# Layers 2 and 3 with value products between the first score blocks, and two of layer 2's expert products formed in layer 1's FFN

## The chip, the cores and the metric

One NeuronCore of one Trainium2 chip runs the whole program as one launch. The metric is the device time of that launch in microseconds, the median of several runs. A core has five engines, each with its own program, which meet only through semaphores: PE (TensorE, matrix products, results to PSUM), ACT (ScalarE), DVE (VectorE), POOL (GpSimd) and SP (SyncE, which here issues the DMAs). The profile lists PE's weight loads apart, as PEld.

## What is computed

The input x holds 8 sequences of 112 tokens with 256 features (896 tokens, 7 tiles of 128). Four layers follow, each a cross-attention to a context of 8 x 375 keys with 192 features and then a feed-forward network (FFN), both behind a layer norm and added to x:

```python
x = x + _L1_xattn_ref(_layernorm(x), ctx, ...)      # 8 heads of 128
x = x + _L1_ffn_ref(_layernorm(x), ...)             # quantised gate, up and down
x = x + _L2_xattn_ref(_layernorm(x), ctx, ...)      # 16 heads of 64
x = x + _L2_ffn_ref(_layernorm(x), ...)             # 8 experts, the best two of each token
x = x + _L3_xattn_ref(_layernorm(x), ctx, ...)      # 16 heads of 64
x = x + _L3_ffn_ref(_layernorm(x), ...)             # 8 experts and a shared one
```

An expert of layer 2 has nothing between its two matrices, so their product doesn't depend on x:

```python
for e in range(E):
    h = xt @ w_in[e].T
    y = y + gates[:, e:e + 1] * (h @ w_out[e].T)
```

The attention of layers 2 and 3 is q = xn Wq, k = c Wk, v = c Wv, softmax(q k^T / 8) v Wo, head by head.

## The kernel before

The program is a row of phases: attention and FFN of layers 0, 1, 2, 3. Each phase ends with a barrier of all engines, and the next begins behind it. Inside a phase an engine's instructions stand in a fixed order, written out by hand. Products that need more than one pass of precision are split in a high and a low part (names that end in H and L), with three to five matmuls for one product: ACT copies the high part out of PSUM, DVE subtracts it to get the low part.

**Layer 1's FFN** (`layer1_ffn`, L1399). DVE computes the layer norm of the 7 tiles, scales and rounds them to `f_xq`; PE turns them (L1550, 14 transposes), ACT copies them out (L1514). Then, tile by tile, PE forms the gate and up products (`up`, L1554, bf16, 8 matmuls of 512 columns in banks 0 to 3), ACT applies silu (L1521), DVE multiplies and finds the maximum (L1475, L1478), ACT scales (L1526), DVE rounds (L1491), PE turns the result (L1566), ACT copies it out (L1531), PE forms the down product (`down`, L1562, in banks 6 and 7 by turns) and DVE adds it to x (L1496). PE's order is up(i+1), down(i-1) for each i; ACT's is gates(i+1), scaled(i), turned_out(i-1). No DMA and no POOL instruction is in this phase.

**Attention of layers 2 and 3** (`attention_heads64`, L1581, called for both). Heads go in 8 pairs h, and in a pair one sequence b after another: 64 steps (h, b), numbered n = 8h + b. For one step PE forms the scores of both heads (L1895, into banks 0 and 1, which every step reuses), DVE the maximum (L2062), ACT the exponentials with their sums (L1976), DVE the reciprocals (L2067), POOL the normalised probabilities (`norm`, L1774); PE turns them (L1905), ACT and DVE take the high and low part out (L1982, L2071), PE multiplies by the values (mix, 9 matmuls) and ACT and DVE take the result out (L1990, L2080). In step n PE issues scores(n+3), turn(n+1), pieces of other work, and mix(n).

The pieces are what step tables (L1594 to L1600) assign: chunks of keys (5 matmuls of 500 columns), halves of queries (6 of 448), units of values (10 of 256; 12 units u for two head pairs), output products, and in layer 2 the products of the experts (`combine`, L1878: 8 matmuls of 128x256 in plain float32 for half an expert (e, j); DVE copies the result, L2055). All of these share three PSUM banks by turns: the m-th piece waits until DVE has emptied the bank of piece m-3. The experts stand in the even head pairs, two each, at steps 1, 3, 5 and 7. The values of head pair 0 stand in steps 0 to 6:

```python
EXPERTS_AT = {1: (0, 0), 3: (0, 1), 5: (1, 0), 7: (1, 1)} if experts else {}
FIRST_VALUES_AT = (None, None, 0, 1, 1, 2, 3, 3, 4, 5, 5, 6)
```

Ahead of the steps stands the start of the phase. SP loads the weights of pair 0 (L1748), POOL cuts them in high and low parts (L1808), DVE computes the layer norm, PE forms five key chunks, with the turning of the normed x between the third and the fourth, then values(0,0), queries(0,0), values(0,1), scores of steps 0, 1 and 2 (L1948), turn(0); then step 0. The queries' second half, (0,1), stands in step 0, and scores of step 4 need it.

**Layer 2's FFN** uses the 8 products `combined` that the attention has left.

## Time and profile before

| what | us |
|---|---|
| median of 3 runs | 1965.8 (1965.56 to 1965.81) |
| the profiled execution | 1964.94 |
| its span in the trace | 1963.1 |
| layer 1's FFN, first instruction of DVE to that of the next phase | 982.1 to 1039.1 |
| layer 2's attention, to its last normalisation | 1039.1 to 1426.2 |
| layer 3's attention, to its last normalisation | 1495.7 to 1826.7 |

Times inside the trace are microseconds from the start of the span; busy time of PE is a modelled end, so matmuls that follow each other overlap, and the start of one to the start of the next is what it costs. PEclk is the clock that the chip granted to TensorE, as a share of 2.4 GHz (0.50 is 1.2 GHz). A timeline row gives start, duration, engine, line, operation, result <- operands, and in brackets the idle time of the engine before it with what ended that.

### The profile page before, as it was taken

How to read it: one execution, taken by the hardware profiler on the slowest of the kernel's cores; microseconds unless marked ns; L12 is line 12 of the kernel's file. 1: busy time of each engine (PE TensorE's matmuls, PEld its weight loads, DVE VectorE, ACT ScalarE, POOL GpSimd, SP SyncE). 2: the span in 40 equal slices, each digit the busy share in tenths (PEclk: the TensorE clock that was granted, in tenths of full speed). 3: DMA queues.
4: the chain of work that ended last, by engine and by line, in shares of the span. 5: the costliest groups of instructions: out<-in, count | busy, mean ns of one | idle time of the engine just before them, and what ended most of it. 6: DMA issues, size and time to landing. Idle time of an engine off the chain costs nothing. (4 is left out here: it accounts for less than half of the span.)

```text
span 1963.1 us, 33822 instructions
## 1 busy us (share of the span) xinstructions
PE 1793.0 (91%) x11747; PEld 1588.6 (81%) x11750; DVE 1420.3 (72%) x3161; ACT 1020.1 (52%) x2243; POOL 507.3 (26%) x533
## 2 busy tenths in 40 slices
PE   6858999999999999999857999999967999999698
PEld 6637999899898989899725888888856888888587
DVE  6478787777777777778676576766676677777786
ACT  3345656465564555656454464655522666666421
POOL 0514030302111120302003233333342334333342
PEclk9988999999999999999978999999989999999899
DMA  4011000000000000000001202020100000000011
GB/s 157 1 75 33 1 12 1 4 8 0 11 0 11 0 11 0 3 0 1 1 1 60 82 28 94 15 94 20 47 1 27 9 15 23 9 10 4 23 54 40
DMA packets 17591, 48.43 MB, mean 25 GB/s; under 512 B 2602, under 2 KB 7347, under 8 KB 15796
## 3 DMA queue, kind: packets, MB, share of 16 engines
q1 hardware_dynamic: 16596, 45.99, 7.1%
q8 instruction: 67, 1.10, 0.2%
...
## 5 line engine op out<-in xcount | busy, mean ns | idle before, releaser
L1280 ACT ACTIVATE a_pH<-banks 125x512 fp32r<-125x512 f32 (+1 forms) x384 | 203.5, 543 | 272.9 <-PE banks L195 192.5
L1351 DVE TENSOR_TENSOR a_pL<-banks,a_pH 125x512 fp32r<-125x512 f32 (+1 forms) x384 | 235.3, 623 | 100.2 <-ACT a_pH L1280 96.5
L1774 POOL TENSOR_TENSOR a_prob<-a_prob,a_rinv 112x750 f32<-112x750 f32 x128 | 183.9, 1437 | 433.7 <-DVE a_rinv L2067 433.7
L1327 DVE TENSOR_SCALAR_CACHE_REDUCE a_prob<-banks 128x500 f32<-128x500 f32 x336 | 223.0, 677 | 17.1 <-issue 12.1
L1181 PE MATMUL banks<-ident,a_prob 128*125 128x128 f32 x1344 | 201.5, 274 | 6.6 <-ACT a_prob L1265 4.4
L195 PE MATMUL banks<-a_pH,a_head_vH 125*128 125x256 f32 (+1 forms) x576 | 203.3, 353 | 2.1 <-DVE a_pL L1351 1.1
L1265 ACT ACTIVATE a_prob<-a_prob,a_nmax 128x1000 f32<-128x1000 f32 x168 | 188.0, 1122 | 28.2 <-DVE a_nmax L1330 28.2
L1181 PEld LDWEIGHTS banks<-ident,a_prob 128*125 128x125 f32 x1344 | 186.9, 188 | 9.9 <-ACT a_prob L1265 4.9
L1137 POOL TENSOR_TENSOR a_head_oH<-a_o,ones 128x256 fp32r<-128x256 f32 (+1 forms) x24 | 16.4, 685 | 624.5 <-DVE a_o L1360 624.5
L195 PE MATMUL banks<-a_pH,a_head_vL 125*128 125x256 f32 (+1 forms) x576 | 173.0, 300 | 0.0
L195 PE MATMUL banks<-a_pL,a_head_vH 125*128 125x256 f32 (+1 forms) x576 | 172.8, 300 | 0.0
L1982 ACT ACTIVATE a_pH<-banks 125x672 fp32r<-125x672 f32 x128 | 93.8, 733 | 128.8 <-PE banks L1905 128.8
L2062 DVE TENSOR_REDUCE a_nmax<-banks 112x2 f32<-112x750 f32 x128 | 119.5, 934 | 45.7 <-PE banks L1895 45.7
L1976 ACT ACTIVATE a_prob<-banks,a_nmax 112x375 f32<-112x375 f32 x256 | 143.8, 572 | 11.9 <-DVE a_nmax L2062 11.9
L195 PE MATMUL banks<-a_head_kH,a_head_qH 128*128 128x500 f32 x336 | 134.6, 401 | 10.8 <-DVE a_prob L1327 9.5
L195 PE MATMUL banks<-a_head_kL,a_head_qH 128*128 128x500 f32 x336 | 131.2, 390 | 0.0
L195 PE MATMUL banks<-a_head_kH,a_head_qL 128*128 128x500 f32 x336 | 130.9, 390 | 0.0
L2071 DVE TENSOR_TENSOR a_pL<-banks,a_pH 125x672 fp32r<-125x672 f32 x128 | 109.8, 858 | 29.1 <-ACT a_pH L1982 27.9
L1905 PEld LDWEIGHTS banks<-ident,a_prob 112*125 112x125 f32 x768 | 95.8, 192 | 33.3 <-issue 33.0
L1990 ACT ACTIVATE a_oH<-banks 64x112 fp32r<-64x112 f32 x256 | 66.0, 258 | 107.2 <-PE banks L195 105.1
L1905 PE MATMUL banks<-ident,a_prob 112*125 112x112 f32 x768 | 118.7, 292 | 0.5 <-DVE a_pL L2071 0.5
L195 PEld LDWEIGHTS banks<-a_pH,a_head_vH 125*128 125x128 f32 x576 | 108.7, 189 | 8.0 <-DVE a_pL L1351 5.2
...
## 6 DMA issues: line engine op xcount, KB each, us to landing
a_w_out<-in_f_out SPq DMA_DIRECT2D x8, 1024.0 KB, 4.9
a_w_in<-in_f_in SPq DMA_DIRECT2D x16, 512.0 KB, 4.7
...
f_quant_raw<-in_f_w SPq DMA_DIRECT2D x3, 1024.0 KB, 7.8
...
```

The costliest lines, as they stand in the source:

```text
L195: last = pe.matmul(out, a, b, start=start and n == 0, stop=stop and n == len(terms) - 1)
L1181: last = pe.transpose(TB[c % 4][0:KB, at:at + P], prob[:, t % RING, key:key + KB], s.ident[:])
L1265: act.activation(row, row, ACT.Exp, bias=nmax[:, t % RING:t % RING + 1], accum_out=rsum[:, t % RING, n:n + 1]).then_inc(exp_done, 1)
L1280: act.activation(pH[:, c % RING, 0:wide], TB[c % 4][0:KB, 0:wide], ACT.Copy).then_inc(t_high, 1)
L1327: dve.tensor_scalar(prob[:, at, c * CHUNK:(c + 1) * CHUNK], SB[c % 3][:, 0:CHUNK], SCALE, None, ALU.mult, ALU.max, accum_out=chunk_max[:, ...
L1351: dve.tensor_tensor(pL[:, c % RING, 0:wide], TB[c % 4][0:KB, 0:wide], pH[:, c % RING, 0:wide].bitcast(F32), ALU.subtract).then_inc(t_done, 1)
L1774: pool.tensor_tensor(both, both, rinv[:, n % RING, :].unsqueeze(2).to_broadcast([SEQ, 2, KEYS]), ALU.mult).then_inc(p_normed, 1)
L1905: last = pe.transpose(T[0:KB, at // BKT, (at % BKT) * SEQ:(at % BKT + 1) * SEQ], probs(n, i)[:, k * KB:(k + 1) * KB], s.ident[0:SEQ, 0:SEQ])
L1976: last = act.activation(probs(n, i), S[0:SEQ, i, own_keys(n % BATCH)], ACT.Exp, bias=nmax[:, n % RING, i:i + 1], accum_out=rsum[:, n % RIN ...
L1982: act.activation(pH[:, n % 2, :].rearrange("p (i c) -> p i c", i=2), T[0:KB, :, 0:HALF], ACT.Copy)\
L2062: dve.tensor_reduce(nmax[:, n % RING, :], S[0:SEQ, :, own_keys(n % BATCH)], AX.X, ALU.max, negate=True).then_inc(max_ready, 1)
L2071: dve.tensor_tensor(pL[:, n % 2, :].rearrange("p (i c) -> p i c", i=2), T[0:KB, :, 0:HALF], pH[:, n % 2, :].rearrange("p (i c) -> p i c", ...
```

## The change

Four things.

1. In both attentions the value units 2 to 9 of head pair 0 leave steps 0 to 5 and stand between the first score blocks: scores(0), three units, scores(1), one unit, turn(0), two units, scores(2), two units. ACT's and DVE's programs follow, DVE with `one_over_sums(0)` behind two low parts. Units 10 and 11 stand in steps 3 and 4.
2. The products of experts 6 and 7 are formed in layer 1's FFN. SP loads both matrices of expert 6 (2 MB) at the start of that phase and those of expert 7 when PE is through with 6. PE forms expert 6's product (16 matmuls) ahead of the transposes of `f_xq`, and expert 7's in four pieces of 4 matmuls, between up(i+1) and down(i-1) for i = 1 to 4. Both use bank 7, ACT copies them out, and layer 1's down product uses bank 6 alone. Head pair 6 of layer 2's attention has no experts any more.
3. The weights of head pair 0 are loaded and cut ahead of the phase that uses them: layer 2's in layer 1's FFN, layer 3's as a ninth pair at the end of layer 2's attention (cut at steps 1 and 2 of pair 7, the values at step 7 of pair 6).
4. `combined` lives from layer 0 on, and the quantised weights of layer 1 lie in its first part.

```diff
@@ -1438,7 +1438,28 @@
+        first_loaded, first_high, first_cut = sem("f1_first_loaded"), sem("f1_first_high"), sem("f1_first_cut")
+        w_in = sb("f1_w_in", [P, KT, EXPERTS, P])
+        w_out = sb("f1_w_out", [P, EXPERTS, D])
+        expert_loaded, e_filled, e_done = sem("f1_expert_loaded"), sem("f1_e_filled"), sem("f1_e_done")
+        EARLY = range(EXPERTS - 2, EXPERTS)
+        PIECE = EXPERTS // 2
...
+        @block.sync
+        def _(sp):
+            for n, e in enumerate(EARLY):
+                if n > 0:
+                    sp.wait_ge(e_filled, KT * n)
+                sp.dma_start(w_out[:], dram["f2_out"][e]).then_inc(expert_loaded, 16)
+                for j in range(KT):
+                    sp.dma_start(w_in[:, j, :, :], dram["f2_in"][e, j]).then_inc(expert_loaded, 16)
+                if n == 0:
+                    first_weights_load(sp, s.pair, dram, 2, first_loaded)
+        @block.gpsimd
+        def _(pool):
+            first_weights_cut(pool, s.pair, first_loaded, first_high, first_cut)
@@ -1493,7 +1514,7 @@
-                dve.scalar_tensor_tensor(s.x[:, i, :], B[6 + i % 2][:, 0:D], ha[:, 3, i:i + 1], s.x[:, i, :],
+                dve.scalar_tensor_tensor(s.x[:, i, :], B[6][:, 0:D], ha[:, 3, i:i + 1], s.x[:, i, :],
@@ -1507,8 +1528,14 @@
+            def combined(n, j):
+                act.wait_ge(e_filled, KT * n + j + 1)
+                act.activation(s.combined[:, EARLY[n], j * D:(j + 1) * D], B[7][:, 0:D], ACT.Copy).then_inc(e_done, 1)
...
+            for j in range(KT):
+                combined(0, j)
@@ -1536,12 +1563,26 @@
+                if i in (3, 5):
+                    combined(1, (i - 3) // 2)
...
+            def combine(n, j, part):
+                pe.wait_ge(expert_loaded, 48 * n + 48)
+                need(pe, e_done, KT * n + j)
+                for k in range(PIECE * part, PIECE * part + PIECE):
+                    last = pe.matmul(B[7][:, 0:D], w_in[:, j, k, :], w_out[:, k, :], start=k == 0, stop=k == EXPERTS - 1)
+                if part == 1:
+                    last.then_inc(e_filled, 1)
+            for j in range(KT):
+                for part in range(2):
+                    combine(0, j, part)
@@ -1566,19 +1607,55 @@
-                need(pe, y_added, i - 1)
-                split_products(pe, B[6 + i % 2][:, 0:D], [
+                need(pe, y_added, i)
+                split_products(pe, B[6][:, 0:D], [
                     (hqT[:, i % 2, k, :], w_down[:, k, :]) for k in range(IT)]).then_inc(y_filled, 1)
...
+                if 1 <= i <= 4:
+                    combine(1, (i - 1) // 2, (i - 1) % 2)
...
+def first_weights_load(sp, w, dram, layer, loaded):
+    sp.dma_start(w.qk_raw[:], dram[f"a{layer}_qk"][0]).then_inc(loaded, 16)
+    sp.dma_start(w.wv_raw[:], dram[f"a{layer}_wv"][0]).then_inc(loaded, 16)
+def first_weights_cut(pool, w, loaded, high, cut):
+    pool.wait_ge(loaded, 32)
+    pool.tensor_copy(w.wH[:], w.qk_raw[:]).then_inc(high, 1)
+    pool.tensor_copy(w.wvH[:], w.wv_raw[:]).then_inc(high, 1)
+    pool.wait_ge(high, 2)
+    pool.tensor_tensor(w.wL[:], w.qk_raw[:], w.wH[:].bitcast(F32), ALU.subtract).then_inc(cut, 1)
+    pool.tensor_tensor(w.wvL[:], w.wv_raw[:], w.wvH[:].bitcast(F32), ALU.subtract).then_inc(cut, 1)
...
@@ -1597,7 +1674,7 @@
-    FIRST_VALUES_AT = (None, None, 0, 1, 1, 2, 3, 3, 4, 5, 5, 6)
+    FIRST_VALUES_AT = {10: 3, 11: 4}
@@ -1613,12 +1690,14 @@
-            return [(0, u) for u, at in enumerate(FIRST_VALUES_AT) if at == b]
+            return [(0, u) for u, at in FIRST_VALUES_AT.items() if at == b]
...
+    LATE = EXPERTS - 2
     def experts_at(h, b):
-        return [(h + EXPERTS_AT[b][0], EXPERTS_AT[b][1])] if h % 2 == 0 and b in EXPERTS_AT else []
+        return [(h + EXPERTS_AT[b][0], EXPERTS_AT[b][1])] if h % 2 == 0 and h < LATE and b in EXPERTS_AT else []
@@ -1632,7 +1711,9 @@
     count("v", (0, 0))
     count("q", (0, 0))
-    count("v", (0, 1))
+    for u in range(1, UNITS):
+        if u not in FIRST_VALUES_AT:
+            count("v", (0, u))
...
@@ -1745,25 +1826,24 @@
-            qk(0)
-            values(0)
             sp.dma_start(bias[:], dram[f"a{layer}_bias"]).then_inc(bias_loaded, 16)
             outs(0)
             if experts:
                 expert(0, 0)
             qk(1)
+            values(1)
             for h in range(HEADS):
                 for b in range(BATCH):
-                    if b == 3 and h + 2 < HEADS:
+                    if b == 3 and h + 2 < PAIRS:
                         qk(h + 2)
-                    if b == 0 and h % 2 == 0 and h // 2 + 1 < HEADS // 2:
-                        values(h // 2 + 1)
+                    if b == 2 and h % 2 == 1 and h // 2 + 2 < (PAIRS + 1) // 2:
+                        values(h // 2 + 2)
                     if b == 4 and h + 1 < HEADS:
                         outs(h + 1)
                     for e, j in experts_at(h, b):
                         if j == 0:
                             expert(e, 1)
@@ -1805,9 +1882,6 @@
-            cut_keys(0)
-            cut_values(0)
-            cut_queries(0)
@@ -1819,13 +1893,13 @@
                         norm(n + 2)
-                    if b == 1 and h + 1 < HEADS:
+                    if b == 1 and h + 1 < PAIRS:
                         cut_keys(h + 1)
-                    if b == 2 and h + 1 < HEADS:
+                    if b == 2 and h + 1 < PAIRS:
                         cut_queries(h + 1)
                     if b == 3 and h >= 1:
                         cut_outs(h)
-                    if b == 7 and h % 2 == 0 and h // 2 + 1 < HEADS // 2:
+                    if b == 7 and h % 2 == 0 and h // 2 + 1 < (PAIRS + 1) // 2:
                         cut_values(h // 2 + 1)
 
@@ -1945,9 +2019,17 @@
             values(0, 1)
-            for b in range(AHEAD):
-                scores(0, b)
+            scores(0, 0)
+            for u in (2, 3, 4):
+                values(0, u)
+            scores(0, 1)
+            values(0, 5)
             turn(0)
+            for u in (6, 7):
+                values(0, u)
+            scores(0, 2)
+            for u in (8, 9):
+                values(0, u)
             for h in range(HEADS):
                 for b in range(BATCH):
@@ -2111,11 +2201,20 @@
             queries(0, 0)
             values(0, 1)
-            for b in range(AHEAD):
-                maxima(b)
-                if b < 2:
-                    one_over_sums(b)
+            maxima(0)
+            for u in (2, 3):
+                values(0, u)
+            one_over_sums(0)
+            values(0, 4)
+            maxima(1)
+            values(0, 5)
             turned(0)
+            one_over_sums(1)
+            for u in (6, 7):
+                values(0, u)
+            maxima(2)
+            for u in (8, 9):
+                values(0, u)
             dve.wait_ge(bias_added, 1)
             for h in range(HEADS):
@@ -2434,17 +2533,17 @@
         s.xnTL = ctx.enter_context(nc.sbuf_tensor("xnTL", [P, KT, TOK], F32R))
-        with ExitStack() as quantised:
-            s.w_quant = quantised.enter_context(nc.sbuf_tensor("w_quant", [P, 3, 2048], BF16))
-            s.w_mean = quantised.enter_context(nc.sbuf_tensor("w_mean", [P, 3], F32))
-            layer0_ffn(nc, s, dram)
-            layer1_attention(nc, s, dram)
+        s.combined = ctx.enter_context(nc.sbuf_tensor("combined", [P, EXPERTS, KT * D], F32))
+        s.w_quant = s.combined[:].rearrange("p e c -> p (e c)").bitcast(BF16)[:, 0:3 * 2048].rearrange("p (n c) -> p n c", n=3)
+        s.w_mean = ctx.enter_context(nc.sbuf_tensor("w_mean", [P, 3], F32))
+        layer0_ffn(nc, s, dram)
+        layer1_attention(nc, s, dram)
+        with ExitStack() as pairs:
+            s.pair = PairWeights(nc, pairs)
             layer1_ffn(nc, s, dram)
-        with ExitStack() as combined:
-            s.combined = combined.enter_context(nc.sbuf_tensor("combined", [P, EXPERTS, KT * D], F32))
-            attention_heads64(nc, s, dram, 2, experts=True)
+            attention_heads64(nc, s, dram, 2, following=3, experts=True)
             layer2_ffn(nc, s, dram)
-        attention_heads64(nc, s, dram, 3)
+            attention_heads64(nc, s, dram, 3)
```

At the start of layer 1's FFN, PE's order before (`f_xq` is the rounded x, `w_quant` the quantised weights):

```order
L1550 MATMUL banks<-f_ident,f_xq 128x128 x14
L195 MATMUL banks<-w_quant,f_xqT 128x512 x24
L1566 MATMUL banks<-f_ident,f_hq 128x128 x8
L195 MATMUL banks<-w_quant,f_hqT 128x256 x8
L195 MATMUL banks<-w_quant,f_xqT 128x512 x8
L1566 MATMUL banks<-f_ident,f_hq 128x128 x8
```

and PE's order there now (the quantised weights go by the name `combined`):

```order
L1579 MATMUL banks<-f_w_out,f_w_in 128x256 x16
L1591 MATMUL banks<-f_ident,f_xq 128x128 x14
L195 MATMUL banks<-combined,f_xqT 128x512 x24
L1579 MATMUL banks<-f_w_out,f_w_in 128x256 x4
L1607 MATMUL banks<-f_ident,f_hq 128x128 x8
L195 MATMUL banks<-combined,f_hqT 128x256 x8
L195 MATMUL banks<-combined,f_xqT 128x512 x8
L1579 MATMUL banks<-f_w_out,f_w_in 128x256 x4
L1607 MATMUL banks<-f_ident,f_hq 128x128 x8
```

Expert 6's 16 matmuls stand ahead of everything, and four of expert 7 ahead of the transposes of each of the first four tiles' hidden values.

At the start of layer 2's attention, DVE's order before, from the maximum of scores(0) on (`a_vL` is a value unit's low part, `a_pL` that of the turned probabilities, `a_qL` that of the queries):

```order
L2062 TENSOR_REDUCE a_nmax<-banks 112x2
L2067 RECIPROCAL a_rinv<-a_rsum 112x2
L2062 TENSOR_REDUCE a_nmax<-banks 112x2
L2067 RECIPROCAL a_rinv<-a_rsum 112x2
L2062 TENSOR_REDUCE a_nmax<-banks 112x2
L2071 TENSOR_TENSOR a_pL<-banks,a_pH 125x672
L2067 RECIPROCAL a_rinv<-a_rsum 112x2
L2062 TENSOR_REDUCE a_nmax<-banks 112x2
```

and DVE's order there now:

```order
L2152 TENSOR_REDUCE a_nmax<-banks 112x2
L2134 TENSOR_TENSOR a_vL<-banks,a_vH 125x512 x2
L2157 RECIPROCAL a_rinv<-a_rsum 112x2
L2134 TENSOR_TENSOR a_vL<-banks,a_vH 125x512
L2152 TENSOR_REDUCE a_nmax<-banks 112x2
L2134 TENSOR_TENSOR a_vL<-banks,a_vH 125x512
L2161 TENSOR_TENSOR a_pL<-banks,a_pH 125x672
L2157 RECIPROCAL a_rinv<-a_rsum 112x2
L2134 TENSOR_TENSOR a_vL<-banks,a_vH 125x512 x2
L2152 TENSOR_REDUCE a_nmax<-banks 112x2
L2134 TENSOR_TENSOR a_vL<-banks,a_vH 125x512 x2
L2157 RECIPROCAL a_rinv<-a_rsum 112x2
```

Eight low parts of values now stand between the maxima and reciprocals of the first three steps.

## Rows read from the trace of the kernel before

**Rows 1.** Windows: busy time of each engine, then granted clock, DMA.

```profile
982.00:1038.00 56.00, 28.77 (x179) 15.96 (x182) 42.05 (x111) 28.61 (x39) 0.00 (x0) 0.79 0.00 1
1000.00:1002.00 2.00, 2.00 (x10) 0.76 (x9) 1.49 (x3) 1.00 (x3) 0.00 (x0) 0.96 0.00 0
1056.84:1074.35 17.51, 11.34 (x61) 9.23 (x62) 7.25 (x12) 7.78 (x21) 4.31 (x3) 0.71 0.01 1
1110.00:1390.00 280.00, 279.21 (x1950) 247.29 (x1949) 184.73 (x361) 157.09 (x421) 94.20 (x90) 1.00 0.17 55
1513.80:1531.50 17.70, 11.54 (x63) 9.40 (x63) 7.26 (x12) 7.76 (x21) 4.31 (x3) 0.71 0.00 0
```

**Rows 2.** Timeline of POOL: normalisations of steps 32 and 48, layers 2 and 3.

```profile
1251.93 1.44 POOL L1774 TENSOR_TENSOR a_prob<-a_prob,a_rinv 112x750 f32<-112x750 f32 x1 [4.60 <-DVE a_rinv L2067]
1344.88 1.44 POOL L1774 TENSOR_TENSOR a_prob<-a_prob,a_rinv 112x750 f32<-112x750 f32 x1 [4.61 <-DVE a_rinv L2067]
1678.65 1.44 POOL L1774 TENSOR_TENSOR a_prob<-a_prob,a_rinv 112x750 f32<-112x750 f32 x1 [4.16 <-DVE a_rinv L2067]
1757.32 1.44 POOL L1774 TENSOR_TENSOR a_prob<-a_prob,a_rinv 112x750 f32<-112x750 f32 x1 [4.16 <-DVE a_rinv L2067]
```

**Rows 3.** Timeline of PE in layer 1's FFN.

```profile
993.96 0.59 PE L1550 MATMUL banks<-f_ident,f_xq 128*128 128x128 bf16 x4 [13.55 <-DVE f_xq L1463]
1009.91 1.89 PE L195 MATMUL banks<-w_quant,f_hqT 128*128 128x256 bf16 x8 [1.12 <-ACT f_hqT L1531]
1026.69 1.89 PE L195 MATMUL banks<-w_quant,f_xqT 128*128 128x512 bf16 x7
1030.59 1.05 PE L195 MATMUL banks<-w_quant,f_hqT 128*128 128x256 bf16 x8 [1.57 <-ACT f_hqT L1531]
```

**Rows 4.** Timeline of ACT in layer 1's FFN, one tile.

```profile
1027.32 1.26 ACT L1521 ACTIVATE f_gate<-banks,f_xa 128x512 f32<-128x512 f32 x2 [1.57 <-PE banks L195]
1029.52 1.02 ACT L1531 ACTIVATE f_hqT<-banks 128x1024 bf16<-128x1024 bf16 x1
```

**Rows 5.** DMA issues of 1096 to 1106 us: KB, us to landing.

```profile
a_w_out<-in_f_out SPq DMA_DIRECT2D x1, 1024.0 KB, 5.0
a_w_in<-in_f_in SPq DMA_DIRECT2D x1, 512.0 KB, 6.0
```

**Rows 6.** Timelines of DVE and POOL: layer norms of two phases.

```profile
982.24 2.38 DVE L96 BATCH_NORM_STATS2 f_ln_stats<-x_stream 128x6 f32<-128x256 f32 x7
986.55 2.35 DVE L118 TENSOR_SCALAR f_xn<-x_stream,f_ln_mean_var,f_ln_root 128x256 f32<-128x256 f32 x7
...
1039.09 2.39 DVE L96 BATCH_NORM_STATS2 a_ln_stats<-x_stream 128x6 f32<-128x256 f32 x7 [0.91 <-PEq L61]
1043.48 1.28 POOL L1798 TENSOR_TENSOR a_wvL<-a_wv_raw,a_wvH 128x512 fp32r<-128x512 f32 x1
1043.58 1.20 DVE L109 SCALAR_TENSOR_TENSOR a_ln_root<-a_ln_root 128x7 f32<-128x7 f32 x1
1045.15 2.84 DVE L118 TENSOR_SCALAR a_prob<-x_stream,a_ln_mean_var,a_ln_root 128x256 f32<-128x256 f32 x7
```

**Rows 7.** Timeline of PE at the start of layer 2's attention.

```profile
1048.69 1.69 PE L164 MATMUL banks<-ident,a_prob 128*128 128x128 f32 x14
...
1056.84 0.42 PE L1895 MATMUL banks<-a_kH,a_qH 64*112 64x376 f32 x2
...
1060.32 0.42 PE L1895 MATMUL banks<-a_kH,a_qH 64*112 64x376 f32 x2 [2.72 <-ACT a_prob L1976]
...
1072.08 0.28 PE L195 MATMUL banks<-a_wvH,ctxH 128*125 128x256 f32 x1
...
1073.26 0.27 PE L195 MATMUL banks<-a_pH,a_vH 125*128 125x224 f32 x1
```

**Rows 8.** Timelines of ACT and DVE there: one value unit taken out.

```profile
1073.46 0.60 ACT L1961 ACTIVATE a_vH<-banks 125x512 fp32r<-125x512 f32 x1 [0.63 <-PE banks L195]
1074.09 0.69 DVE L2044 TENSOR_TENSOR a_vL<-banks,a_vH 125x512 fp32r<-125x512 f32 x1 [0.61 <-ACT a_vH L1961]
```

75 lines of the change are left out of this document (45 added, 30 removed).

## Prediction

> **What bounds the kernel now.** I read the windows by stage first. In the middle of layer 2's attention PE is busy 279.2 of 280 us at clock 1.00 [rows 1]: there PE sets the time, and a matmul taken out is time gained. The start of each attention is of another kind. From layer 2's first scores to those of step 4 PE is busy 11.34 of 17.51 us at mean clock 0.71, and layer 3's start shows the same, 11.54 of 17.70 [rows 1]: 6.2 us idle, and as a mean of 0.71 says that 58% of the stretch ran at 1.2 GHz instead of 2.4, some 3.6 us more go to half speed (3.3 if idle and busy time were evenly mixed). The timeline of PE says why: scores(1) start 3.48 us behind scores(0), after 2.72 us idle for ACT's exponentials [rows 7], since all scores share one pair of banks. Layer 1's FFN is the third kind: PE is busy 28.8 of 56 us and DVE 42.1, in chains through all engines, and POOL and DMA do nothing [rows 1]. So the change moves work from where PE is full to where it has room, and the question is what it costs there.
>
> **Part 1, products in layer 1's FFN: a loss.** SP starts the 2 MB of expert 6 with the phase, at about 982.1 (DVE's norm begins at 982.24 [rows 6]). The nearest transfers, 1 MB and 0.5 MB, landed 5.0 and 6.0 us after their issues, and the second was issued some 0.4 us later, so 0.5 MB takes about 1.4 us; 2 MB land at 982.1 + 6.4 + 1.4 = 989.9 [rows 5].
>
> What does a product cost? Two equal blocks of two head pairs, in layer 2 with experts and in layer 3 without, take 1344.88 - 1251.93 = 92.95 and 1757.32 - 1678.65 = 78.67 us [rows 2]. All else in them is the same work, so four half-expert products of 8 matmuls cost 14.28, and one 3.57, at full clock. In the FFN the first meets a PE that has been idle for 13.55 us [rows 3]. Before, PE began there at 993.96 [rows 3] and had full clock only from 1000.1 on (mean 0.96 in the window from 1000 [rows 1]), with gaps in its work. The products leave no gap; between 0 and 6.1 us of half speed I take 3, which lose 1.5. Product one ends at 989.9 + 3.57 + 1.5 = 995.0. The second waits for ACT to copy bank 7, at most the 0.60 of its 512-column copies [rows 8], and ends at 999.2. The transposes that began at 993.96 begin 5.4 us later with a hand-over; from 4 (no half speed) to 8 (6.1 us of it).
>
> Then the loop over tiles. At full clock it takes 4.78 us and runs up 1026.69, silu 1027.32, scaling, turned copy 1029.52 to 1030.54, down product 1030.59 to 1031.47 [rows 3, 4]. PE's own way through it is up and transposes 1030.59 - 1026.69 - 1.57 = 2.33, then 1.1 for ACT's copy behind them, then down 0.88: 4.3. Four matmuls of expert 7 (half of 3.57, 1.79) between up and transposes make it 6.1, longer than the loop: 1.3 us each for i = 2, 3, 4. At i = 1 the piece lies in the wait for DVE's rounding. So +3.9. At i = 3 the piece also waits for ACT's copy of the half before it, which stands behind silu and scaling of the next tile: 0.63 + 2.2 + 0.4 behind up's start, where up itself takes 1.7: +1.5. ACT's copy at i = 5 stands ahead of the turned copy: +0.4. Against that a busier PE keeps its clock: a down product of 8 matmuls took 1.89 at 1009.91 and 1.05 at 1030.59 [rows 3], and it, the up product behind it and the transposes ahead of both would lose 2.5 us less. The loop costs 3.9 + 1.5 + 0.4 - 2.5 = +3.3. Down products in bank 6 alone cost nothing: DVE's addition of 256 columns, under the 0.69 that it took for 512 [rows 8], is done while PE turns the next tile and ACT copies it. Expert 7's load starts at 999.2 and lands some 8 us later, ahead of its first piece at about 1011. **Layer 1's FFN: 5.4 + 3.3 = +8.7**, bounds +6 and +14 (both halves half as dear again).
>
> POOL's cut of the first weights moves here as well, to about 991 to 995, where DVE scales and rounds x. In layer 2's norm a DVE instruction on 7 columns took 1.20 us beside POOL's subtraction of 1.28, and ended with it [rows 6]. With 1.28 for each of two subtractions and half that, an estimate, for each of two copies, DVE could be held up by 3.8 us in all, and `f_xq`, for which PE waited until 993.96 [rows 3], come at 997.8. PE isn't through with expert 6 until 999.2: cost nothing, and up to 3.8 if that cover were gone. The Trainium skill (SBUF — State Buffer, "SBUF: two separate sides") calls the port pair of DVE and GpSimd an exclusive lock for which the loser waits a whole instruction; the trace agrees. By it the moved cut is no cheaper in the FFN than in the attention, only better covered, and the sum stays as it is.
>
> **Part 2, weights ahead: a gain at both starts.** From its first to its last instruction the norm takes 982.24 to 988.90, 6.66 us, with POOL silent, and 1039.09 to 1047.99, 8.90 us, beside POOL's cuts [rows 6]: 2.2 us go. PE's first key chunks no longer wait for a cut, so the turning of xn, 0.7 behind the norm's end (1048.69 [rows 7]), follows it at once. The 8.15 us from there to the first scores [rows 7] are a chain through all engines, and stay. Gain 2.2 + 0.6, less 0.2 for a PE that may be slow in the turning: **2.6** in layer 2, 2.7 in layer 3. Bounds 1 (half speed through turning and keys) and 3.2.
>
> **Part 3, values between scores.** A unit takes 1.18 us of PE (1072.08 to 1073.26 [rows 7]), 0.60 of ACT and 0.69 of DVE [rows 8]. The stretch to scores(4) held one unit and now holds 8: 7 x 1.18 = 8.2 us leave the full steps behind it. How much longer does the stretch get? Its work at full clock was 17.5 - 6.2 - 3.6 = 7.7, now 15.9. Idle time left: scores(0) and three units (4.2) cover the 3.48. turn(0) waits, since DVE's reciprocal stands behind two low parts: 3.48 + 3 x 0.65, then POOL's 1.44 [rows 2], is 6.9 or 7.0 against PE's 6.1: 0.9. scores(3) wait for exponentials whose maximum stands on DVE behind a low part, a turned part, a reciprocal and two more low parts: 1.0. scores(4) wait for the queries' second half, whose low part stands behind the maximum and exponentials of step 3: 1.6. With 3.5 idle the stretch takes 19.4, and the gain is 17.5 + 8.2 - 19.4 = 6.3. PE's clock fell there in its idle time and I take it to stay up. The steps behind must not be thinner than their own chain: one with a key chunk alone holds about 3.6 us of PE against a chain of 3.5 [rows 7], so I take off 0.2 in layer 2 and 0.5 in layer 3: **6.1 and 5.8**; bounds 3 (half of the wait stays) and 9 (no idle time).
>
> **Part 4, layer 2's pair 6 without experts.** 14.3 us of PE go [rows 2]; five steps with little left may lose 0.1 each, and layer 3's first weights put a cut of at most two times 1.28 [rows 6] into two steps of pair 7, behind normalisations of 1.44 [rows 2]. **-13.8**, bounds 12.5 and 14.3. SP's loads go past nothing that is late.
>
> **Sum** against the profiled execution: 1964.9 + 8.7 - 2.6 - 6.1 - 13.8 - 2.7 - 5.8 = 1942.6. The median of before lies 0.9 above that execution, so 1943.5.
>
> **Rivals.**
> (A) The fill gives little: low parts of values stand ahead of maxima and reciprocals on DVE, and high parts ahead of exponentials on ACT, so the chain of each step grows by two or three of 0.65 us and scores wait as before. For it: PE waits there for ACT [rows 7]. Against: DVE is busy 7.25 of 17.51 us [rows 1]. A gain of 3 in place of 6 in each layer: 1949.5.
> (B) The FFN costs 14, its bound, since the 2 MB land late or POOL outlasts its cover: 1949.
> (C) Both go better: no idle time among the scores, and fast products: -3 in each layer, -1.5 in the FFN: 1936.
> (D) Slower than before: PE stays at 1.2 GHz through layer 1's FFN. The first two products take 14.3 us, and the transposes start 10.8 later; a tile with a piece takes 4.7 (up, transposes) + 3.6 + 1.1 + 1.8 = 11.2 against 4.78, three times +6.4, the other three +2.8; ACT's copies +1.9: about +40 in place of +8.7, 1975. It decides if the clock does not come up at the products or is lost again among the tiles. Against it: the stage had full clock from its middle on, with less work (1.05 at 1030.59 [rows 3]). The Trainium skill (TensorE: Matmul & The Clock Gate, Part 1) has the gate set by how busy PE has been of late, which speaks against (D) too.
> (E) It doesn't come to anything: fills that do nothing and an FFN that takes back the experts' gain, within 4 us of before.
>
> **How the numbers follow.** Forecast 0.60, A 0.14, B 0.11, C 0.10, D 0.02, E 0.03. The likeliest gives 1943.5; the range reaches from C's 1936 to past A and B, 1952. A measurement tells about 0.2% (4 us) from no change: faster 0.95, same 0.03, slower 0.02.
>
> **What would show it.** Layer 1's FFN: product rows from 990, first transposes near 999.4 instead of 993.96, next phase at about 1048 instead of 1039.1. Both attentions: norms of 6.7 instead of 8.9 us, 19.4 us from the first scores to scores(4) at a clock near 1.00 with three gaps of 1 to 1.6. Layer 2's pair 6 shorter by 14 us. I am wrong if the FFN grows by over 14, if the stretch of first scores takes over 22 us, or if pair 6 gives back less than 12.

## The result, and the profile after

| kernel | median us | runs | ratio to before (95%) |
|---|---|---|---|
| before | 1965.7 | 1963.1 to 1965.8 | 1 |
| after | 1936.95 | 1933.8 to 1939.6 | 0.9856 (0.9839 to 0.9873) |

The change gains 28.7 us where 22.3 were forecast. The time lies inside the range, 6.5 us below the likeliest case and beside rival C's 1936. The profiled execution took 1937.66, its span 1935.7, 27.4 less than before's.

A phase begins here at the first row of its layer norm, and the norm of step n is POOL's normalisation of that step. All are in us; each column is one profiled execution.

| stretch | before | after | difference | forecast |
|---|---|---|---|---|
| up to layer 1's FFN (untouched) | 982.24 | 981.33 | -0.9 | 0 |
| layer 1's FFN | 56.85 | 67.38 | +10.5 | +8.7 |
| layer 2's attention, start to first scores | 17.75 | 14.04 | -3.7 | -2.6 |
| layer 2's scores(0) to scores(4); the difference counts the 8.2 of values moved in | 17.51 | 18.66 | -7.05 | -6.1 |
| norm of step 48 to norm of step 63 (pair 6 in it) | 79.89 | 66.04 | -13.85 | -13.8 |
| layer 3's attention, up to its FFN | 340.07 | 328.73 | -11.3 | -8.5 |
| norm of step 63 to layer 3's attention, and layer 3's FFN (untouched) | 70.95, 127.31 | 71.79, 125.3 | -1.2 | 0 |

The windows after, to be read against [rows 1] (busy time of PE, PEld, DVE, ACT, POOL with counts, then granted clock, DMA share, GB/s). First the whole of layer 1's FFN, its last 7.7 us, the first scores of layer 2, the middle of layer 2's attention, the first scores of layer 3:

```profile
981.33:1048.71 67.38, 44.66 (x243) 29.18 (x247) 45.20 (x111) 29.88 (x44) 3.71 (x4) 0.83 0.19 71
1041.00:1048.71 7.71, 4.63 (x24) 3.03 (x25) 0.97 (x2) 1.50 (x3) 0.00 (x0) 0.50 0.00 0
1062.75:1081.41 18.66, 17.03 (x132) 15.08 (x133) 11.75 (x20) 11.70 (x30) 4.32 (x3) 1.00 0.01 1
1120.00:1400.00 280.00, 279.06 (x1976) 246.77 (x1974) 191.37 (x375) 164.39 (x444) 100.65 (x98) 1.00 0.13 42
1495.69:1514.36 18.67, 17.03 (x132) 15.08 (x133) 11.75 (x20) 11.71 (x30) 4.32 (x3) 1.00 0.00 1
```

The first scores are what was meant: PE busy 17.03 of 18.66 us at full clock, where it was 11.34 of 17.51 at 0.71. In layer 3 the same stretch took 17.70 before [rows 1] and 18.67 after, so its gain is 7.23. The middle is as full as before. The FFN ends at a clock of 0.50, which I had not foreseen.

PE in layer 1's FFN after, against [rows 3]: both products, the first transposes, the third piece, and the last three down products.

```profile
989.05 5.32 PE L1579 MATMUL banks<-f_w_out,f_w_in 128*128 128x256 f32 x16 [9.54 <-DMA f_w_in<-in_f_in]
994.93 3.69 PE L1579 MATMUL banks<-f_w_out,f_w_in 128*128 128x256 f32 x16 [0.56 <-ACT combined L1533]
998.46 0.39 PE L1591 MATMUL banks<-f_ident,f_xq 128*128 128x128 bf16 x4
...
1023.63 1.97 PE L1579 MATMUL banks<-f_w_out,f_w_in 128*128 128x256 f32 x8 [1.46 <-ACT combined L1533]
...
1038.29 1.05 PE L195 MATMUL banks<-combined,f_hqT 128*128 128x256 bf16 x8 [1.84 <-ACT f_hqT L1558]
...
1041.49 1.89 PE L195 MATMUL banks<-combined,f_hqT 128*128 128x256 bf16 x8 [1.12 <-ACT f_hqT L1558]
...
1045.35 1.89 PE L195 MATMUL banks<-combined,f_hqT 128*128 128x256 bf16 x8 [1.12 <-ACT f_hqT L1558]
```

PE is idle for 9.54 us until the load has landed; the 1 MB took 5.3 us from issue to landing and each 0.5 MB of `f_w_in` 6.6, against 5.0 and 6.0 in [rows 5]:

```profile
f_w_out<-in_f_out SPq DMA_DIRECT2D x1, 1024.0 KB, 5.3
f_w_in<-in_f_in SPq DMA_DIRECT2D x2, 512.0 KB, 6.6
```

The transposes start 17.13 us behind the phase's start where they started 11.72 behind it. DVE in the same place: POOL's cut of layer 2's first weights ran from 990.32 to 994.11, and the scaling of x took 4.03 us. The first row is the same scaling before the change, with POOL silent: 1.93 us.

```profile
991.67 1.93 DVE L1459 TENSOR_SCALAR f_big<-f_xn,f_xa 128x256 f32<-128x256 f32 x7
```

```profile
991.55 4.03 DVE L1480 TENSOR_SCALAR f_big<-f_xn,f_xa 128x256 f32<-128x256 f32 x7
995.49 1.49 DVE L1484 TENSOR_SCALAR f_xq<-f_big 128x256 bf16<-128x256 f32 x7
```

The start of layer 2's attention, against [rows 6] and [rows 7]: DVE's last normalisation, then PE's turning of xn, the first scores and scores(4).

```profile
1053.03 2.35 DVE L118 TENSOR_SCALAR a_prob<-x_stream,a_ln_mean_var,a_ln_root 128x256 f32<-128x256 f32 x7
...
1054.49 1.69 PE L164 MATMUL banks<-ident,a_prob 128*128 128x128 f32 x14
...
1062.75 0.42 PE L1969 MATMUL banks<-a_kH,a_qH 64*112 64x376 f32 x2
...
1076.44 0.43 PE L1969 MATMUL banks<-a_kH,a_qH 64*112 64x376 f32 x2 [0.33 <-ACT a_prob L2058]
...
1081.41 0.44 PE L1969 MATMUL banks<-a_kH,a_qH 64*112 64x376 f32 x2 [1.13 <-DVE a_qL L2127]
```

Layer 2's pairs 6 and 7, by POOL's normalisations of steps 48 and 63, against [rows 2] (before's step 48 stands there, at 1344.88; its step 63 was at 1424.77):

```profile
1343.84 1.44 POOL L1854 TENSOR_TENSOR a_prob<-a_prob,a_rinv 112x750 f32<-112x750 f32 x1 [4.62 <-DVE a_rinv L2157]
...
1409.88 1.44 POOL L1854 TENSOR_TENSOR a_prob<-a_prob,a_rinv 112x750 f32<-112x750 f32 x1 [2.44 <-DVE a_rinv L2157]
```

The windows between those two steps, before and then after: PE is busy 13.85 us less, and idle for 1.99 us in both.

```profile
1344.88:1424.77 79.89, 77.90 (x537) 68.06 (x534) 51.90 (x104) 43.70 (x123) 25.90 (x24) 1.00 0.11 36
```

```profile
1343.84:1409.88 66.04, 64.05 (x473) 55.83 (x470) 49.77 (x100) 43.46 (x123) 30.00 (x29) 1.00 0.03 7
```

### The profile page after: what moved, and what is told of

Same layout as the page of the kernel before. It is cut to its first block and busy times, and to the rows that moved or that the text cites. A ratio compares the mean times of both kernels' runs of the same rounds, so it can differ in the third digit from the quotient of the medians.

```text
span 1935.7 us, 33792 instructions
## 1 busy us (share of the span) xinstructions
PE 1793.0 (93%) x11747; PEld 1585.4 (82%) x11750; DVE 1410.4 (73%) x3157; ACT 1020.4 (53%) x2247; POOL 507.4 (26%) x531
## 5 line engine op out<-in xcount | busy, mean ns | idle before, releaser
L195 PE MATMUL banks<-a_pH,a_vH 125*128 125x224 f32 x384 | 107.7, 281 | 7.2 <-DVE a_oL L2170 7.1
```

The costliest lines, as they stand in the source:

```text
L195: last = pe.matmul(out, a, b, start=start and n == 0, stop=stop and n == len(terms) - 1)
```

## Experiments: one part at a time

**e1, the fill alone**: before, with `FIRST_VALUES_AT = {10: 3, 11: 4}` and the new order in front of the steps (PE's part of it is shown; ACT and DVE follow).

```diff
+            scores(0, 0)
+            for u in (2, 3, 4):
+                values(0, u)
+            scores(0, 1)
+            values(0, 5)
             turn(0)
+            for u in (6, 7):
+                values(0, u)
+            scores(0, 2)
+            for u in (8, 9):
+                values(0, u)
```

> The kernel before with nothing changed but the order of head pair 0's values: units 2 to 9 between the first score blocks, in layers 2 and 3. In the changed kernel's trace the stretch from scores(0) to scores(4) took 18.66 us against 17.51 with 7 x 1.18 us more work in it, so this edit by itself should give 7.0 us in each layer: 1965.7 - 14.1 = 1951.6. Rival: the stretch was short there only since PE came to it after an undisturbed start; then 4 to 5 us in each layer, 1956. A second rival, that the fill by itself holds the scores back (my case A): 3 in each layer, 1960.

Measured: 1949.95 (1947.98 to 1950.73), before 1964.0; ratio 0.9924 (0.9907 to 0.9940), a gain of 14.1; the two stretches of the changed kernel gave 7.05 and 7.23. scores(0) to scores(4) take 1057.27 to 1075.94, 18.67 us, and 18.67 in layer 3, the same as in the changed kernel, whose norms and loads are other ones. The fill stands by itself. The two larger waits that are left, ahead of scores(3) and scores(4), are the same too:

```profile
1070.97 0.42 PE L1897 MATMUL banks<-a_kH,a_qH 64*112 64x376 f32 x2 [0.35 <-ACT a_prob L1986]
...
1075.94 0.43 PE L1897 MATMUL banks<-a_kH,a_qH 64*112 64x376 f32 x2 [1.12 <-DVE a_qL L2055]
```

Layer 1's FFN is here the code from before the change, and yet its clock fell at the end: its last two down products took 1.62 and 1.89 us, and the phase took 58.24 us in place of 56.85.

```profile
1027.94 1.05 PE L195 MATMUL banks<-w_quant,f_hqT 128*128 128x256 bf16 x8 [1.57 <-ACT f_hqT L1531]
...
1031.36 1.62 PE L195 MATMUL banks<-w_quant,f_hqT 128*128 128x256 bf16 x8 [1.12 <-ACT f_hqT L1531]
...
1034.95 1.89 PE L195 MATMUL banks<-w_quant,f_hqT 128*128 128x256 bf16 x8 [1.12 <-ACT f_hqT L1531]
```

**e2, the experts alone**: the changed kernel without the fill and without the weights ahead.

```diff
-                if n == 0:
-                    first_weights_load(sp, s.pair, dram, 2, first_loaded)
...
+            cut_keys(0)
+            cut_values(0)
+            cut_queries(0)
```

> The kernel before with only the products of experts 6 and 7 moved into layer 1's FFN. That phase took 56.85 us before and 67.38 in the changed kernel, layer 2's pair 6 gives back 13.8: 10.5 - 13.8 = -3.3, 1962.4. If the extra 1.8 us over my sum (8.7) is TensorE's clock falling at the end of the phase, this kernel shows 1.2 GHz rows there too, or a phase of 65.5 us where it doesn't. Rival: the phase's extra length comes from the weights' loads and cuts moved there as well, then 8.7 here, 1960.6.

Measured: 1961.85 (1958.86 to 1965.18, ten runs); ratio 0.9990 (0.9981 to 1.0000). The FFN takes 65.45 us, +8.6, with all its down products at 1.05 us. The gain is 2.2 us against the before measured beside it (1964.04), with an interval that ends at no gain: what pair 6 gives back, the FFN takes for the most part. By itself this run can't tell a fallen clock from the rival (the weights' loads and cuts), since both would leave 8.7. Two runs below can: e8 has these loads and cuts, no fallen clock, and 65.53 us; e4 has no cut in this phase, a fallen clock, and 67.67 us. It is the clock.

**e3, the weights ahead alone**: the changed kernel without the fill and without experts in layer 1's FFN.

```diff
-                sp.dma_start(w_out[:], dram["f2_out"][e]).then_inc(expert_loaded, 16)
...
-            for j in range(KT):
-                for part in range(2):
-                    combine(0, j, part)
```

> The kernel before with only the weights of head pair 0 loaded and cut ahead of the phase. In the changed kernel the first scores of layers 2 and 3 came 3.7 and 4.05 us sooner after the start of the norm: -7.7, 1958.0. Theory of the port: as no 2 MB go ahead of them, the weights land about 2.6 us after the start of layer 1's FFN and POOL cuts them beside that phase's layer norm, which becomes 2.2 us longer (8.9 instead of 6.66) with nothing to cover it: 1960.2. Rival: the norm in layer 1's FFN stays at 6.7 us, and 1958.0.

Measured: 1958.05 (1954.42 to 1958.74); ratio 0.9966 (0.9952 to 0.9981). The median is the rival's number, but the before measured beside it was 1964.04 and not 1965.7: the gain is 6.0, between the 5.5 of the theory and the 7.7 of the rival, and its interval holds both. The trace decides, and it shows the longer norm. Without 2 MB ahead of them the weights land early, and POOL's cut falls on the layer norm. The norm of the FFN takes 9.07 us instead of 6.66, which is 2.4 of the 2.9 by which the FFN is longer (59.74 instead of 56.85). DVE and POOL there:

```profile
981.00 0.52 DVE L109 SCALAR_TENSOR_TENSOR f_ln_root<-f_ln_root 128x7 f32<-128x7 f32 x1
...
981.75 4.12 DVE L118 TENSOR_SCALAR f_xn<-x_stream,f_ln_mean_var,f_ln_root 128x256 f32<-128x256 f32 x7
...
981.58 1.26 POOL L1638 TENSOR_TENSOR pair_wL<-pair_qk_raw,pair_wH 128x512 fp32r<-128x512 f32 x1
982.80 1.31 POOL L1639 TENSOR_TENSOR pair_wvL<-pair_wv_raw,pair_wvH 128x512 fp32r<-128x512 f32 x1
```

The starts of both attentions gain 3.7 and 4.0. So the parts alone are worth 14.1, 2.2 and 6.0, in all 22.3, and together 28.7. Of the 6.4 between them up to 2.9 are this cut: beside the experts it costs nothing, since PE isn't through with expert 6. The rest isn't apportioned. Stretches that no edit reaches differ by as much between two profiles: in e2's, what follows the norm of step 63 took 73.82 us against 70.95 before, scores(0) to scores(4), without the fill, 18.77 and 18.83 against 17.51 and 17.70, and what lies ahead of layer 1's FFN 2.2 less.

**e4, the cut back in the phase that uses it**, the loads left ahead.

```diff
-            first_weights_cut(pool, s.pair, first_loaded, first_high, first_cut)
+            pool.wait_ge(first_loaded, 32)
...
+                pool.tensor_copy(high_part, raw).then_inc(zero_high, 1)
+                pool.wait_ge(zero_high, m + 1)
+                pool.tensor_tensor(low_part, raw, high_part.bitcast(F32), ALU.subtract).then_inc(zero_cut, 1)
```

> The changed kernel with the first weights still loaded ahead, but cut by POOL at the start of the attention that uses them (both layers). It tells apart what the start gained from, the load or the cut. If it was POOL beside DVE, the norm is long again, 8.9 us, and the first scores come 2.2 us later than in the changed kernel in each layer: 1941.4. If it was waiting for the DMA, the norm's length changes nothing and the first scores stay within 0.5 us: 1938. As POOL now starts with the norm, beside instructions that it may not hold up (the statistics), something between is likely: norm 7.5, 1939.5.

Measured: 1936.72 (1935.98 to 1937.54); ratio 0.9860 (0.9844 to 0.9877) against the changed kernel's 0.9856, so the median doesn't tell the two apart. The trace does: the first scores come 14.61 and 14.45 us behind the phase's start instead of 14.04 and 14.02, some 0.5 later, where before had 17.75 and 18.07, and the norm takes 7.06 us, 0.4 more. That is the case in which the load was what mattered. With nothing to wait for POOL starts with the phase, and is through at 1050.50, before DVE's tile-wide instructions begin:

```profile
1046.25 2.38 DVE L96 BATCH_NORM_STATS2 a_ln_stats<-x_stream 128x6 f32<-128x256 f32 x7 [0.94 <-PEq L61]
1050.95 2.35 DVE L118 TENSOR_SCALAR a_prob<-x_stream,a_ln_mean_var,a_ln_root 128x256 f32<-128x256 f32 x7
...
1048.06 1.28 POOL L1897 TENSOR_TENSOR pair_wvL<-pair_wv_raw,pair_wvH 128x512 fp32r<-128x512 f32 x1
1049.29 0.39 POOL L1895 CAST pair_wH<-pair_qk_raw 128x256 fp32r<-128x256 f32 x1
1049.76 0.74 POOL L1897 TENSOR_TENSOR pair_wL<-pair_qk_raw,pair_wH 128x256 fp32r<-128x256 f32 x1
```

So 3.1 of 3.7 us and 3.6 of 4.05 come from the load and not from the place of the cut: the load had put the cut beside DVE's tile-wide work.

## Experiments: what layer 1's FFN pays for

**e5, PE kept busy at the FFN's end.**

```diff
+                if i >= TILES - 3:
+                    pe.wait_ge(g_done, 2 * TILES)
+                    for _ in range(4):
+                        pe.matmul(B[0][:, :], xqT[:, 0, 0:P], w_gate[:, 0, 0:512], start=True, stop=True)
                 pe.wait_ge(ht_done, i + 1)
```

> The changed kernel with four matmuls of 512 columns, whose result nobody reads, behind the transposes of each of the last three down products of layer 1's FFN, where PE otherwise waits for ACT's copy. Theory: in the profile of the changed kernel PE's clock falls to 0.50 some 8 us before that FFN ends, the last two down products take 1.89 instead of 1.05 us and layer 2's first key chunks 0.62 instead of 0.39, in all some 1.9 us in the FFN. The run without weights ahead had the FFN at 65.45 us with all down products at 1.05. Expected: FFN 65.5 us in place of 67.4, median 1935 in place of 1937, a smaller spread of the runs. Rival: whether the clock falls there is not decided by what the FFN does at its end; then the down products are as likely as before to take 1.89, and the median stays within 1 us.

Measured: 1934.03 (1933.16 to 1939.57), ratio 0.9844 (0.9831 to 0.9858). The FFN takes 64.61 us, all its down products 1.05, and layer 2's key chunks 0.39 from the first. So in this profile the clock stayed up as the theory has it (with PE's code as it was it did so too in e2's and e8's profiles, so one profile doesn't prove the cause); the median isn't told apart from the changed kernel's 0.9856, and the runs spread as before, so the end of this FFN is not what spreads them.

**e6, ACT's copies one tile earlier.**

```diff
-                if i in (3, 5):
-                    combined(1, (i - 3) // 2)
                 if i >= 1:
                     turned_out(i - 1)
+                if i in (2, 4):
+                    combined(1, (i - 2) // 2)
```

> The changed kernel, with ACT's two copies of expert 7's halves behind its turned copy of tiles 1 and 3, one tile earlier than in the changed kernel. Theory: PE's wait of 1.46 us for the copy ahead of the third piece (i = 3) is ACT's order alone, as my step had it (1.5), and the copy ahead of the turned copy at i = 5 costs 0.4: FFN 1.9 us shorter, 65.5 with a fallen clock. Rival: the loop over tiles is then held by the next thing in the chain (DVE's rounding) and gives back under 0.7.

Measured: 1935.43 (1932.91 to 1936.67), ratio 0.9842 (0.9828 to 0.9855). The FFN takes 65.31 us in place of 67.38, with the clock fallen at its end as in the changed kernel; the wait of 1.46 is gone. That is 2.07 us less where 1.9 were expected: these waits were ACT's order. The median isn't told apart from the changed kernel's.

**e7, the products where PE waits.** The main parts of the edit; `PIECES` gives for each down product which half-expert product is worked on, from which matmul to which. Beside what is shown, all loads start with the phase, with a semaphore and a buffer for each half.

```diff
+        PIECES = {0: (2, 0, 2), 1: (2, 2, 5), 2: (2, 5, 8), 3: (3, 0, 3), 4: (3, 3, 6), 5: (3, 6, 8)}
...
-                sp.dma_start(w_out[:], dram["f2_out"][e]).then_inc(expert_loaded, 16)
+                sp.dma_start(w_out[:, n, :, :], dram["f2_out"][e]).then_inc(half_loaded[KT * n], 16)
...
+            pool.wait_ge(scales_ready, 2)
             first_weights_cut(pool, s.pair, first_loaded, first_high, first_cut)
...
-            for j in range(KT):
-                for part in range(2):
-                    combine(0, j, part)
+            combine(0, 0, 8)
...
+            combine(1, 0, 2)
             pe.wait_ge(xt_done, TILES)
...
-                if 1 <= i <= 4:
-                    combine(1, (i - 1) // 2, (i - 1) % 2)
+                if i <= 1:
+                    combine(1, (2, 4)[i], (4, 8)[i])
...
                 last.then_inc(ht_filled, 1)
+                if i in PIECES:
+                    combine(*PIECES[i])
                 pe.wait_ge(ht_done, i + 1)
```

> The changed kernel, with the products in layer 1's FFN placed anew: only expert 6's first half ahead of the transposes, waiting for 1.5 MB in place of 2; the other 24 matmuls in pieces of two to four where PE waits (2 behind the transposes of x, 2 and 4 behind up 1 and 2, and 2 or 3 between the transposes and the product of down 0 to 5, beside ACT's copy); buffers for both experts, so that all 4 MB load at once; POOL's cut of the first weights moved behind the rounding of x, beside DVE's wait for the first up product. Theory: the FFN's 10.5 us are the transposes held up by 5.4 and pieces that lie outside PE's waits (3.9 + 1.9), not the products' 14.3 us as such; PE's waits of 0.9 to 1.95 hold all 24. Expected: transposes at phase + 12.3 in place of 17.1, FFN 57 us (55.5 to 59) in place of 67.4, median 1927 (1925 to 1929.5). Rival: the pieces lengthen the chain of each tile since the down product waits behind them (each piece of three takes 1.34 against a wait of 1.1), or 4 MB arrive too late: FFN 61 us or more, median 1931 or more.

Measured: 1922.87 (1921.15 to 1926.51), ratio 0.9786 (0.9772 to 0.9799). The FFN takes 54.45 us, 12.9 less than in the changed kernel, and 2.4 less than before the change, with 14.3 us more work in it, but at a mean clock of 0.91 where before had 0.79. First its window, then PE: product one, the transposes at phase + 12.36, one tile's piece beside ACT's copy, the last down product.

```profile
976.37:1030.82 54.45, 41.75 (x243) 27.72 (x247) 42.00 (x111) 29.35 (x44) 3.65 (x4) 0.91 0.23 88
...
982.66 6.23 PE L1584 MATMUL banks<-f_w_out,f_w_in 128*128 128x256 f32 x16 [8.13 <-DMA f_w_in<-in_f_in]
988.73 0.39 PE L1594 MATMUL banks<-f_ident,f_xq 128*128 128x128 bf16 x4
...
1010.51 0.61 PE L1611 MATMUL banks<-f_ident,f_hq 128*128 128x128 bf16 x8
1010.95 1.51 PE L1584 MATMUL banks<-f_w_out,f_w_in 128*128 128x256 f32 x6
1012.68 1.05 PE L195 MATMUL banks<-combined,f_hqT 128*128 128x256 bf16 x8 [0.22 <-ACT f_hqT L1559]
...
1028.28 1.05 PE L195 MATMUL banks<-combined,f_hqT 128*128 128x256 bf16 x8 [1.12 <-ACT f_hqT L1559]
```

A piece of three matmuls stands in a wait that was 1.57 us [rows 3] and leaves 0.22 of it. DVE is busy 42.00 us instead of 45.20: POOL's cut, now behind the rounding of x, holds nothing up.

**e10 and e11** take e7 apart. e10 puts both halves of expert 6 ahead of the transposes again; e11 moves expert 7's pieces back between up and transposes as well. The first cut shows e10 against e7, the second e11 against e10.

```diff
             combine(0, 0, 8)
+            combine(1, 0, 8)
...
-            combine(1, 0, 2)
...
-                if i <= 1:
-                    combine(1, (2, 4)[i], (4, 8)[i])
```

> As e7, but both halves of expert 6 ahead of the transposes of x; expert 7's pieces stay beside ACT's copies. Tells what the hold-up of the transposes is worth by itself. Theory: a matmul ahead of the transposes delays the whole FFN one to one: transposes at phase + 16.4 (3.6 for the product, 0.5 for its load), FFN 54.5 + 4.1 - 0.9 (six matmuls fewer among the up products, whose waits they only partly filled) = 57.7, median 1926. Rival: the FFN is bounded behind its start by the chain of DVE and ACT, and takes the hold-up back: 55.5 or less, median 1923.5.

```diff
+                if 1 <= i <= 4:
+                    combine(2 + (i - 1) // 2, (0, 4)[(i - 1) % 2], (4, 8)[(i - 1) % 2])
...
-                if i in PIECES:
-                    combine(*PIECES[i])
```

> As e10, with expert 7's four pieces of four matmuls back between the up product and the transposes, behind up 2 to up 5, as in the changed kernel, ACT's copies behind its turned copies of tiles 1 and 3. Against e10 it moves the 16 matmuls and nothing else. Theory: three of four pieces lie on PE's chain, 1.3 us each by my step: FFN 57.7 + 3.9 less what down 0 to 5 lose by e10's pieces (0.2 each) = 60.5 to 61.5, median 1929. Rival: the place among a tile's instructions does not matter, PE has the same work: FFN within 1 us of e10.

Measured: e10 1930.14 (1929.44 to 1930.54), ratio 0.9821, where 1926 was expected; e11 1934.45 (1933.73 to 1936.29), ratio 0.9846, where 1929 was. e10's FFN is 1.6 us longer than the 57.7 expected, and e11's 2.8 longer than the upper end of its 60.5 to 61.5.

| kernel | FFN, us | transposes at phase + | mean clock |
|---|---|---|---|
| before | 56.85 | 11.72 | 0.79 |
| after | 67.38 | 17.13 | 0.83 |
| e2 | 65.45 | 17.43 | 0.90 |
| e6 | 65.31 | 17.23 | 0.85 |
| e11 | 64.27 | 16.55 | 0.85 |
| e10 | 59.31 | 16.49 | 0.88 |
| e7 | 54.45 | 12.36 | 0.91 |

```profile
979.43:1038.74 59.31, 43.45 (x246) 28.70 (x247) 42.09 (x112) 29.47 (x44) 3.65 (x4) 0.88 0.21 80
```

e7 to e10 is 4.9: the transposes come 4.1 later, one to one, and in the first tile, where PE has waited 1.94 us again, a piece of two matmuls takes 2.02 instead of 1.10; I had subtracted 0.9 for a fuller tile loop, and that didn't come. e10 to e11 is 5.0, more than the 3 to 4 expected. A tile with a piece takes 6.07 us in e11 (down at 1008.99 and 1015.05) and 4.78 in e10 (1015.82 and 1020.60): 1.3 for each of three, as my step had it. The clock falls in e11 at the end and not in e10: the last three down products there follow each other by 3.43 and 3.86 us and not by 3.42 and 2.61, and the phase ends 0.8 later behind the last. Against that the first down product comes 0.8 sooner in e11. The rival, that the place doesn't matter, is out by 4 us. From e6 (65.31) to e11 (64.27), both with a fallen clock, the earlier loads, the second buffer and POOL's later cut come together; they weren't taken apart.

**e8, the queries' second half earlier.**

```diff
             scores(0, 2)
-            for u in (8, 9):
-                values(0, u)
+            queries(0, 1)
+            values(0, 8)
```

> The changed kernel, with the queries' second half ahead of value unit 8, before step 0, and value unit 9 in step 0 in its place, in both attentions. Theory: scores(4) waited 1.13 us for DVE's low part of these queries, which stood behind the maximum and the reciprocal of step 0; it goes. Expected: 17.5 us in place of 18.66 from scores(0) to scores(4), 1.1 us less in each layer, median 1935. Rival: scores(4) then wait for the exponentials of scores(3), which the trace has just behind the queries: under 0.4 per layer, no change that shows.

Measured: 1931.51 (1930.01 to 1933.65), ratio 0.9827 (0.9814 to 0.9840). scores(4) wait for nothing any more, and scores(0) to scores(4) take 17.54 us in both layers, 1.12 less:

```profile
1057.78 0.43 PE L1970 MATMUL banks<-a_kH,a_qH 64*112 64x376 f32 x2
...
1071.47 0.42 PE L1970 MATMUL banks<-a_kH,a_qH 64*112 64x376 f32 x2 [0.30 <-ACT a_prob L2059]
...
1075.32 0.42 PE L1970 MATMUL banks<-a_kH,a_qH 64*112 64x376 f32 x2
```

The median fell by more than the two stretches give, 5.4 against 2.2. In e8's profile the FFN, whose code is the changed kernel's, took 65.53 us without the fall of the clock; whether that is chance or comes of the edit stays open.

**e9, e7 and e8 together.**

> The products spread over PE's waits (as in e7) and the queries' second half ahead of value unit 8 (as in e8) together. The two touch different stretches: layer 1's FFN at 54.5 us, 17.54 us from scores(0) to scores(4) in both layers. Expected: 1922.9 less 2 x 1.12 = 1920.6, between 1918 and 1922.5; the gain over before 2.3%. Rival: one of the two medians owed something to the clock of other phases, and both together come out at 1923.

Measured: 1922.18 (1919.16 to 1925.00), ratio 0.9780 (0.9767 to 0.9793), against e7's 0.9786. Its trace has both: an FFN of 54.43 us and 17.54 from scores(0) to scores(4), twice. The 2.2 us more that this should give can't be told in the median from none. In its profile layer 2's FFN, which the edit doesn't reach, took 2.1 us more than in e8's (the stretch from the norm of step 63 to the next phase; e8 first, then e9):

```profile
1403.71:1474.99 71.28, 53.60 (x248) 41.22 (x247) 53.10 (x112) 9.46 (x20) 20.20 (x19) 0.88 0.00 0
```

```profile
1392.92:1466.34 73.42, 55.78 (x249) 42.70 (x247) 53.14 (x113) 9.47 (x20) 20.20 (x19) 0.86 0.00 0
```

The same work in 248 and 249 rows of PE, busy 2.2 us longer at a lower clock. e7 and e9 are 14 and 15 us faster than the changed kernel.

## Why the prediction was right, and where it wasn't

**The direction and the parts** were right: the loss in the FFN, the gains at both starts, at the first scores and in pair 6 are each in the trace with their sign, and layer by layer within 2 us of their size. The sum was 6.4 us short of the gain: starts (2.4), first scores (2.4) and phases left alone (2.1) gave more than forecast, the FFN 1.8 less; 1.3 is how medians stand to profiles. The 2.1 and the 1.3 come from nothing that I had worked out, and each column of the table is one execution, so the parts' own numbers carry such differences too.

**Layer 1's FFN, +8.7, was +10.5.** Point by point: the load's end, forecast for 989.9 by before's clock, came 7.7 us behind the phase's start (forecast 7.7). Product one with its cold clock took 5.32 + 0.56 to the second, where my step had 5.1 + 0.6 (in the other profiles with this code the first product took 5.33 to 6.61), and the transposes were held up by 5.41, where it said 5.4. Pieces of 1.3 each, the wait of 1.5 (1.46) and the copy of 0.4 (e6: both together 2.07) stood as worked out. What did not hold is the clock: "against that a busier PE keeps its clock", -2.5. It did so up to about 1040, when the pieces were over and tiles held only transposes, a wait and a down product; then the clock was 0.50 up to the end, the last two down products took 1.89, and 1.9 of the 2.5 were given back. e2, e5 and e8 show the FFN without that, 65.45, 64.61 and 65.53: +8.6, +7.8 and +8.7. But the 56.85 to which all of these are compared is one execution too: in e1 the same code lost its clock at the end and took 58.24. Against that one the changed kernel's 67.38 and e4's 67.67, with the clock fallen as well, are +9.1 and +9.4. So with the clock alike at the end the phase grew by 8.6 to 9.4, and the fall itself, 1.4 to 1.9 us, is nothing that the change brought: I had taken the end of one trace for certain.

**The cover of POOL's cut** was called for at up to 3.8 us and costless. DVE was held up by 3.2 (busy 45.20 against 42.00 in e7), its rounding ran from 995.49 to 996.98, PE took the first tile at 998.46. e3 shows the price without the cover, 2.9 us in the FFN. The Trainium skill (SBUF — State Buffer, "SBUF: two separate sides") gives the lock only to a DVE instruction in a 2-port mode or with two SBUF inputs, and has the loser wait out a whole instruction of the other engine. The trace agrees that instructions differ: the tile-wide arithmetic took 4.12 beside POOL's casts and subtractions and 2.35 alone, while the seven batch-norm statistics, which read one tensor, took 2.38 in e4 beside POOL's cut as they do alone.

**Starts of the attentions, -2.6 and -2.7, were -3.7 and -4.05.** The norm shrank as worked out (8.90 to 6.67). What failed is "the turning follows the norm's end at once". It doesn't wait for the end: it started at 1054.49, while DVE's last normalisations ran from 1053.03 to 1055.38, since it takes tiles as they come. Before, it had been kept from that by key chunks that waited for the cut: it started 0.7 behind the norm's end. That makes some 1.5 us beside the 2.2 of the norm. Starting it still sooner gives nothing: in e5 and e7, with key chunks at full clock, it began 5.1 us behind the phase's start and not 5.8, and the first scores came at 14.04 as here. The size of the gain hangs on before's trace as well: without the weights ahead the first scores came 16.86 to 18.99 us behind the phase's start (before, e1, e2), with them at 14.02 to 14.05 in every profile with the cut ahead too.

**The fill, -6.1 and -5.8, was -7.05 and -7.23.** I had three waits of 0.9, 1.0 and 1.6; the trace has 0.17, 0.33 and 1.13, at the same three places. So the term that was mis-sized is the idle time, 3.5 against 1.6. I had added the chains of ACT, DVE and POOL end to end; that they are shorter in sum is measured, which steps overlap wasn't taken apart. Part of the gain was lost again, for the work at full clock was 17.03 us and not 15.9: 7.7 had been worked out from a mean clock, and is 8.8. The clock stayed up, as assumed.

**Pair 6, -13.8, was -13.85.** In a stretch where PE is nearly always busy a matmul taken out is its own length. That the sum came out to 0.1 is partly luck: the four half-expert products were 13.85 us of PE's busy time and not the 14.28 from the two equal blocks [rows 2], and the 0.5 that I took off for steps with little left shows nowhere, as PE is idle for 1.99 us before and after. The price from the blocks was good to 3%.

**Rivals.** A (3 us per layer) fell by e1. B (FFN at +14) fell: the load landed when it was to. D fell: the clock came up at the products; but its mechanism, a clock lost among thin tiles, is what took 1.9 us at the end. E fell with the size of the gain. C's number was met by other terms than C's own: no idle time among scores (there is 1.6) and a faster FFN (it was slower). Of the span's 27.4 us, 2.1 lie in phases that the change doesn't touch; the last 1.3 of the 28.7 are how the medians stand to the two profiled executions.
